# Decoder layer on one core: order of bank reads in the attention's reading cycles, and the last block's first steps placed inside the last attention cycles

## What is computed

```python
x = layernorm(x + attn(x))     # polynomial terms of a gate and a SwiGLU of width 1248
x = layernorm(x + xattn(x))    # 32 heads of width 128
x = layernorm(x + ffn(x))      # SwiGLU of width 1376

# xattn
h_q = rmsnorm(x) @ w_q.T; h_k = ctx @ w_k.T; h_v = ctx @ w_v.T
score = einsum('bqhd,bkhd->bhqk', h_q, h_k) + position_bias
score = softmax(where(mask, score, -inf))
out = x + einsum('bhqk,bkhd->bqhd', score, h_v) @ w_out.T

# ffn (the last block)
out = (silu(x @ Wg.T * ag) * (x @ Wu.T * au)) @ Wd.T * ad
```

## Time and profile before

| | |
|---|---|
| median of three runs | 755.46 us |
| the profiled execution's own time | 753.72 us |
| span of its profile (first to last instruction) | 751.9 us |
| TensorE busy | 716.2 us (95%), granted clock 0.992 on average |
| VectorE busy | 522.2 us (69%) |
| ScalarE busy | 408.6 us (54%) |
| GpSimd busy | 94.8 us (13%) |
| attention, from about | 206 to 612 us |
| last block, from | 613.1 us |

### The profile page before, as it was taken

How to read it: one execution, slowest core, us unless ns; L and a number is a source line. 1 busy time by engine, 2 the same in 40 slices (tenths; PEclk the granted TensorE clock), 3 DMA queues, 4 the chain that set the end, 5 groups by cost and what they waited for, 6 DMA issues and landing times.

```text
span 751.9 us, 12237 instructions
## 1 busy us (share of the span) xinstructions
PE 716.2 (95%) x4082; PEld 555.7 (74%) x4082; DVE 522.2 (69%) x848; ACT 408.6 (54%) x747; POOL 94.8 (13%) x88
## 2 busy tenths in 40 slices
PE   8999999999999999999999999999999779998993
PEld 6788888888878878776667787877656257886882
DVE  6555687588664875686876678667897828669565
ACT  6333323432355676776776666666676644454552
POOL 2000000074003600000000000000050004105403
PEclk9999999999999999999999999999999999999997
DMA  8455532545556765677997776668785513442631
GB/s 307 152 206 206 179 119 70 163 168 187 183 208 199 251 195 181 216 258 233 306 316 236 240 238 190 192 215 267 263 297 180 169 44 117 135 151 98 204 122 56
DMA packets 70681, 145.10 MB, mean 193 GB/s; under 512 B 7920, under 2 KB 8192, under 8 KB 69984
## 3 DMA queue, kind: packets, MB, share of 16 engines
q1 hardware_dynamic: 69200, 137.26, 55.7%
q0 software_dynamic: 1200, 6.70, 2.3%
q10 hardware_dynamic: 224, 0.39, 0.2%
HBM read 142.23 MB, written 2.10 MB: 192 GB/s over the span
## 4 chain that ended last, share of the span: by engine, by line
PE 86%; DVE 5%; issue 3%; DMA 2%; ACT 2%; POOL 1%; SPq 0%; ACTq 0%; DVEq 0%; POOLq 0%
PE bank L543 38%; PE acc L543 16%; PE acc L846 8%; PE bank L751 7%; PE bank L824 7%; PE bank L716 7%; PE bank L778 1%; PE bank L729 1%; DMA b_raw<-b 1%; DMA a_raw<-a 1%; PE bank L575 1%; DVE tile_lo L1288 1%; ACT v_sb L1186 1%; DVE a_lo L1288 1%; DMA wq<-wqn 1%
## 5 line engine op out<-in xcount | busy, mean ns | idle before, releaser
L543 PE MATMUL bank<-feat_hi,a_hi 128*128 128x512 f32 x348 | 137.7, 396 | 2.2 <-ACT u_sb L1193 0.8
L543 PE MATMUL bank<-feat_lo,a_hi 128*128 128x512 f32 x348 | 136.5, 392 | 2.1 <-issue 2.1
L1288 DVE TENSOR_TENSOR a_lo<-a_raw,a_hi 128x1024 fp32r<-128x1024 f32 (+3 forms) x47 | 56.8, 1208 | 94.5 <-ACT a_hi L1000 86.9
L543 PE MATMUL acc<-b_hi,tile_hi 128*128 128x512 f32 x224 | 87.8, 392 | 4.9 <-DVE tile_lo L1288 3.0
L543 PE MATMUL acc<-b_hi,tile_lo 128*128 128x512 f32 x224 | 87.3, 390 | 0.0
L543 PEld LDWEIGHTS bank<-feat_hi,a_hi 128*128 128x128 f32 x348 | 65.9, 189 | 22.6 <-issue 4.0
L543 PEld LDWEIGHTS bank<-feat_lo,a_hi 128*128 128x128 f32 x348 | 65.9, 189 | 13.5
L846 PE MATMUL acc<-u_sb,prob_t 32*128 32x512 f32 x512 | 73.0, 640 | 0.0
L543 PE MATMUL bank<-feat_hi,a_lo 128*128 128x512 f32 x180 | 70.1, 389 | 0.0
L1017 ACT ACTIVATE tile_hi<-pair 128x512 fp32r<-128x512 f32 x54 | 33.9, 628 | 66.3 <-DVE pair L1350 37.4
L751 PEld LDWEIGHTS bank<-t_ring,xn 128*128 128x128 f32 x512 | 62.1, 192 | 8.5 <-issue 7.2
(11 more groups left out here) (152 smaller groups left out, 1555.8 us busy)
## 6 DMA issues: line engine op xcount, KB each, us to landing
wqi<-ax SPq DMA_DIRECT2D x64, 256.0 KB, 3.3
wq<-wqn SPq DMA_DIRECT2D x64, 256.0 KB, 3.7
wv<-wvh SPq DMA_DIRECT2D x64, 256.0 KB, 4.0
wo<-bx SPq DMA_DIRECT2D x64, 256.0 KB, 4.0
a_raw<-w SPq DMA_DIRECT2D x22, 512.0 KB, 4.1
wk<-ax SPq DMA_DIRECT2D x43, 256.0 KB, 3.8
a_raw<-a SPq DMA_DIRECT2D x21, 512.0 KB, 5.4
b_raw<-b SPq DMA_DIRECT2D x34, 256.0 KB, 2.7
```

The costliest lines, as they stand in the source:

```text
L543: mm = pe.matmul(out_ap, w, x, start=start and k == 0, stop=stop and k == len(products) - 1, skip_group_check=True)
L1288: return dve.tensor_tensor(out_ap, whole, high, ALU.subtract)
```

## The change

Four things are done.
- In reading cycles TensorE's `values(n)` stands right behind `turn(n-1)` and no longer waits for `turned_ok`; ScalarE copies v_sb ahead of u_sb.
- `FEATURES_2` is HN - 6 = 58: the features' chunks 0, 1 and 2 stand in cycle 58, chunk 3 at the head of cycle 59, with their parts on ScalarE and VectorE. Since k_ring may still be in use, they are written to new tiles `last_hi`, `last_lo`, which share the addresses of ctx_raw1 and xn1 for half 0 and are feat_hi[1], feat_lo[1] for half 1.
- `gate(A30)` stands at the end of cycle 61 and `up(A30)` at the end of cycle 62, into bank 2 instead of bank 1. Silu follows in ScalarE's cycle 62, its split of weight tile A30 + 1 in cycle 61.
- SyncE loads A30 + 1 and T30 in cycle 58.

```diff
-FEATURES_1, FEATURES_2 = BLOCK - LEAD_T - 2, HN - 2
+FEATURES_1, FEATURES_2 = BLOCK - LEAD_T - 2, HN - LEAD_T
+GATE_30, UP_30 = HN - 3, HN - 2
...
# SyncE, at the end of a cycle
+                if n == FEATURES_2:
+                    sp.wait_ge(t_mm, HN)
+                    load_a(A30 + 1, (A30 + 1) % 2, w3[1][:, 0:2 * D])
+                    load_b(T30, T30 % 2, w3[0][:, 2 * D:])
-            sp.wait_ge(t_mm, HN)
...
# TensorE
-            def up(par, half, done, low=True):
+            def up(par, half, done, low=True, last=False, into=bank[1]):
                 pe.wait_ge(hidden_ok, done)
-                project(bank[1], par, 1, half, low=low).then_inc(a_used, 1)
+                project(into, par, 1, half, low=low, last=last).then_inc(a_used, 1)
...
# TensorE, values(n)
-                    else:
+                    elif shared(n) or not few:
                         pe.wait_ge(turned_ok, n)
...
# TensorE, a cycle
                     if n == HN:
                         weigh(n - 2)
-                        pe.wait_ge(feat_lo_ok, C)
-                        gate(A30, A30 % 2, 0, HALVES * F1)
+                    if n == FEATURES_2 + 1:
+                        features(2, 3, resid[:, TT:2 * TT, :], HN)
                     if n >= 1:
                         turn(n - 1)
+                    if few and late:
+                        values(n)
                     if 2 <= n < HN:
                         weigh(n - 2)
...
-                    if n >= FEATURES_2 and n < HN:
-                        features(2, 2 * (n - FEATURES_2), resid[:, TT:2 * TT, :], HN)
+                    if n == FEATURES_2:
+                        features(2, 0, resid[:, TT:2 * TT, :], HN)
...
                     if late:
                         outer(n - 1)
-                    if 0 <= n < HN:
+                    if 0 <= n < HN and not late:
                         values(n)
...
+                    if n == FEATURES_2:
+                        features(2, 1, resid[:, TT:2 * TT, :], HN)
...
+                    if n == GATE_30:
+                        pe.wait_ge(feat_lo_ok, C)
+                        gate(A30, A30 % 2, 0, HALVES * F1, last=True)
+                    if few and n == UP_30:
+                        pe.wait_ge(added_ok, HN)
+                        up(A30 % 2, 0, HALVES * F1, last=True, into=bank[2])
                     if few and 1 <= j <= 2 and 0 <= g and g + 1 < HALVES * GROUPS:
                         group_scores(g + 1, j - 1)
+                    if n == FEATURES_2:
+                        features(2, 2, resid[:, TT:2 * TT, :], HN)
...
                 pe.wait_ge(u_ok, HN)
-                up(A30 % 2, 0, HALVES * F1)
                 weigh(HN - 1)
...
# ScalarE, a cycle
+                if n == FEATURES_2 + 1:
+                    chunk(2, 3, bank[0])
                 if n >= 1:
                     copy_turned(n - 1)
...
-                if n >= FEATURES_2:
-                    chunk(2, 2 * (n - FEATURES_2), bank[0])
+                if n == FEATURES_2:
+                    chunk(2, 0, bank[0])
...
+                if n >= 0:
+                    copy_values(n)
                 if late:
                     copy_outer(n - 1)
-                if n >= 0:
-                    copy_values(n)
...
+                if n == FEATURES_2:
+                    chunk(2, 1, bank[0])
                 if 0 <= n + 1 < HN:
                     exponentials(n + 1)
+                if n == FEATURES_2:
+                    chunk(2, 2, bank[0])
...
+                if n == GATE_30:
+                    act.wait_ge(score_mm, HN)
+                    split_a(A30 + 1, (A30 + 1) % 2)
+                if n == UP_30:
+                    silu(A30, HALVES * F1, True, 0)
...
-            silu(A30, s0, True, 0)
+            split_b(T30, T30 % 2)
             copy_turned(HN - 1)
             copy_outer(HN - 1)
-            split_a(A30 + 1, (A30 + 1) % 2)
-            split_b(T30, T30 % 2)
...
# VectorE, a cycle
                 if 0 <= m < HN and m % GH > 0:
                     find_max(m)
+                if n == FEATURES_2:
+                    chunk(2, 0, bank[0])
+                if n == FEATURES_2 + 1:
+                    chunk(2, 3, bank[0])
                 if n >= 0:
                     divide(n)
...
-                if n >= FEATURES_2:
-                    chunk(2, 2 * (n - FEATURES_2), bank[0])
-                    chunk(2, 2 * (n - FEATURES_2) + 1, bank[0])
+                if n == FEATURES_2:
+                    chunk(2, 1, bank[0])
+                    chunk(2, 2, bank[0])
...
-            product(A30, s0, T30, T30 % 2, True, 0)
+            product(A30, s0, T30, T30 % 2, True, 0, second=bank[2])
```

More of the change, by code:

```diff
@@ L545, in passes, with project @@
                 return mm
-            def project(bank_, par, which, half, x_hi=feat_hi, x_lo=feat_lo, low=True):
+            def project(bank_, par, which, half, low=True, last=False):
+                x_hi, x_lo = (last_hi, last_lo) if last else (feat_hi, feat_lo)
                 for c in range(C):
@@ L576, in transposes, with gate @@
                 mm.then_inc(feat_mm, 1)
-            def gate(a, par, half, done, low=True):
+            def gate(a, par, half, done, low=True, last=False):
                 pe.wait_ge(a_lo_ok, a + 2)
                 pe.wait_ge(silu_ok, done)
-                project(bank[0], par, 0, half, low=low).then_inc(first_mm, 1)
-            def up(par, half, done, low=True):
+                project(bank[0], par, 0, half, low=low, last=last).then_inc(first_mm, 1)
+            def up(par, half, done, low=True, last=False, into=bank[1]):
                 pe.wait_ge(hidden_ok, done)
-                project(bank[1], par, 1, half, low=low).then_inc(a_used, 1)
+                project(into, par, 1, half, low=low, last=last).then_inc(a_used, 1)
             for h in range(HALVES):
@@ L899, in attention @@
                         down(T30 - 1, (T30 - 1) % 2, 1, last=True)
+                    if not few and late:
+                        values(n)
                     if late:
                         outer(n - 1)
-                    if 0 <= n < HN:
+                    if 0 <= n < HN and not late:
                         values(n)
@@ L954, in last_block @@
                 transposes(3, 1, bank[3], x1)
-                gate(a, a % 2, 0, s0 + f, low=low)
+                gate(a, a % 2, 0, s0 + f, low=low, last=True)
                 pe.wait_ge(feat_lo_ok, C + 1)
@@ L959, in last_block @@
                 transposes(3, 3, bank[3], x1)
-                up(a % 2, 0, s0 + f, low=low)
+                up(a % 2, 0, s0 + f, low=low, last=True)
                 down(T30 + f - 1, (T30 + f - 1) % 2, 5, low=low)
@@ L965, in last_block @@
                 a, t = A30 + F3, T30 + F3
-                gate(a, a % 2, 1, s0 + F3, low=low)
-                up(a % 2, 1, s0 + F3, low=low)
+                gate(a, a % 2, 1, s0 + F3, low=low, last=True)
+                up(a % 2, 1, s0 + F3, low=low, last=True)
                 down(t - 1, (t - 1) % 2, 5, last=True, low=low)
@@ L1341, in few_bias_rests, with product @@
                         few_bias_hi[:, part * GH:(part + 1) * GH, :].bitcast(F32)).then_inc(few_bias_ok, 1)
-            def product(a, done, m, mpar, last_block, f):
+            def product(a, done, m, mpar, last_block, f, second=bank[1]):
                 dve.wait_ge(silu_ok, done + 1)
```

39 lines of the change are left out of this document (22 added, 17 removed).

## The result

The changed kernel took 756.38 us (median of 20 runs, 754.73 to 757.92), the kernel before 755.32 (20 runs): ratio 1.0019, 95% interval 1.001 to 1.0028. The forecast was 753.4, at most 755.2. The profiled execution of after took 757.53 us (span 755.7), 1.2 over its median; that of before was 1.6 under its own. So the two traces lie 3.8 us apart, the medians 1.1. The granted clock of the changed kernel's 20 runs is 0.983 to 0.989 on average, and the profiled one stands at 0.983: it is one of those with the most time at half clock. I follow the traces and judge by the medians.

What follows compares the result with a forecast made beforehand. TensorE was taken as the bound (86% of the chain), VectorE full in cycles 48 to 52. Gains of 2.5 + 1.7, less 0.7 in the tail and 1.5 for the clock, gave 2.0 us: 753.4, range 751.6 to 755.2.

Steps and rivals of the forecast that it cites:

- the last block starting differently from before: Entry to the last block: a sign that would prove the prediction wrong; no change was forecast there.
- Term of 2.5 us for cycles 17 to 32: Cycles 17, 20, 21, 24 and 32: the early copy removes turn's wait for v_ok, five times 0.5 us.
- what is late next?: Reading cycles without the stall: TensorE's own work takes 3.1 us, and ScalarE's copies at 2.9 us just keep up.
- the `sem_inc` that the prediction named as free: Between queries and turn: the added sem_inc costs nothing, as others already stand there without a bubble.
- The second rival: Reading cycles: another wait, exponential chain or weight loads, replaces v_ok; gain about 0.2 to 0.7 us, time 755.0, chance 0.17.
- Term of 1.7 for cycles 53 to 57: Entering cycle 58: 0.7 us from the earlier exponential and k_ring copy, 1.0 from the stalls of cycles 56 and 57.
- Tail: Cycles 58 to 63, features, gate and up moved: loses 0.7 us, with a 3.2 us gap ahead of turn(60).
- the clock's 1.5: Cycle 61, behind the 3.2 us gap: 3.4 us at half clock cost between 0 and 1.7 us, taken as 1.5.
- The sentence on the clock: Cycles' idle gap: low clock is the default, activity lifts it; gain 2.0 us by this rule, 3.5 without.
- The rival "slower": From 593 on the clock stays down; if until weigh(63), it costs 7.5 us and gives 759.5, chance 0.06.

Runs made afterwards that it cites:

- experiments 6 and 8: 6: early copy without keys' idle wait, branch ahead of turn(63), on the kernel before, 748.08 us; 8: changed kernel, branch behind up in cycle 62, 749.63 us.
- Experiment 1: The changed kernel with the wait for u_ok in keys skipped where keys does nothing: 757.64 us, ratio 1.0028.
- experiments 7 and 9: 7: changed kernel, VectorE's feature chunks behind the divisions, 752.51 us, single run; 9: that plus keys' idle wait skipped and branch behind up, 746.19 us.
- experiment 4: The kernel before with the early copy of v_sb and without the u_ok wait where keys does nothing: 751.52 us, ratio 0.9961.
- filler kernel: The changed kernel with twelve matmuls that nobody reads added behind weigh(63): 753.17 us, ratio 0.9981.

## Why the prediction was wrong

- **The step that failed** is the one that had no term: "the last block starting differently from before" stands in the list of what would prove it wrong, and the sum took it at nothing. The text counted up's 2.95 us as work that fills idle time inside the cycles and never asked what those 2.95 us had covered where they stood. They had covered the flag's load and the branch. The timeline held the answer in its next line: the 0.67 us marked "issue" ahead of the gate was the visible end of a stretch of 4.76, from up's first matmul at 608.38 to the gate at 613.14. What the runs showed in its place is a stretch of 4.2 to 5.0 us that only queued matmuls hide; with the branch moved forward (experiments 6 and 8) the idle piece is gone and the time falls by 3.4 and about 7 us. How the stretch divides between the load of the flag, the branch and the fetch of code stays open. Price: 2.7 us by the first idle piece (4.49 against 1.81 from weigh(63) to the gate), and 1.2 between the gate and the mark (14.99 against 13.76), where the clock was low for 10 us instead of 3.4. Both are read from the two profiled executions, which lie further apart than the medians.
- **Term of 2.5 us for cycles 17 to 32**: mis-sized. From the turn of cycle 16 to that of cycle 32 the traces show 79.93 and 78.49 us, 1.44. The question "what is late next?" was answered by TensorE's own work; it was the wait in `keys`, right ahead of the `sem_inc` that the prediction named as free. Experiment 1 shows that. The second rival had said that another wait takes the place of `v_ok`; it was half right, with another wait than the ones it named. The weight loads that it named came next, once that wait was gone.
- **Term of 1.7 for cycles 53 to 57**: mis-sized too, 1.05. From turn(52) to turn(57) it is 23.05 and 22.00 us. (That VectorE ran without a gap from 533.97 on is right but for one piece of 0.16 us at 548.09.)
- **Tail**: right. +2.0 for +0.7 and the clock's 1.5; the idle piece 3.12 for 3.2, the wait at weigh(62) 0.78 for 0.9, one fall of the clock in cycle 61. The table load lay beside up and cost nothing.
- **The sentence on the clock**: the rule of the Trainium skill ("TensorE: Matmul & The Clock Gate", Part 1), that the low clock is the default and activity lifts it, was weighed at the cycles alone. The traces agree with it there, and at the entry too, where the same kind of piece (3.34 us) came with some 10 us at half clock, from 614 to 624. The rival "slower" had the clock as its mechanism, but at the wrong place, and it was not what began it.
- **The size at the end**: by the ratio the loss is 0.8 to 2.1 us, by the profiled executions 3.8. The difference of 2.7 is that of the two executions against their medians (1.60 and 1.15). Against the 751.7 us that the prediction gave for the profiled execution, the 757.53 are 5.8 too much: 3.9 at the entry, 1.6 in the cycles, 0.4 ahead of them, 0.1 behind the mark, less 0.2 in the tail.

## What to carry to other kernels

Before work is moved away from the end of a stage, look at what stands behind it on the same engine that shows no busy time: a flag's load, a branch, code that has to be fetched. A run-time branch on the critical engine goes where several microseconds of its work are already queued, at the price of having that work's code in both branches. And a removed wait is worth only what the next wait in program order lets through: read the code between the removed wait and the instruction, also where that code "does nothing".

## What the runs showed of the hardware

- TensorE's program runs ahead of its matmuls, by some 3 to 4 us at least (the matmuls of up and weigh, or of weigh and the filler): with twelve matmuls more between the last wait and the branch, the first matmul behind it came 4.77 us after that wait, not 3 us later.
- The clock's fall doesn't follow from the length of one idle piece. Pieces of 2.63 us and more ahead of turn(60) came with it in each of seven kernels. The same piece of 1.88 us was followed by 1.00 in the kernels of experiments 7 and 9 and by 0.50 in that with the keys' wait kept, and at the entry a piece of 2.38 us was followed by 1.00 in the kernel of experiment 4, one of 2.13 us by 0.50 in the kernel before. Slices of the kernel with the keys' wait kept:

```profile
591.00:592.00 1.00, 0.34 (x5) 1.00 0.57 217
592.00:593.00 1.00, 1.00 (x9) 0.54 0.03 8
593.00:594.00 1.00, 1.00 (x9) 0.50 0.00 0
```

- At half clock the matmuls of the last block's gate start 0.43 us apart, at full clock 0.23 (changed kernel, 619.44 to 623.71 and 624.76 to 626.14).
- The second idle piece at the entry (2.13 us before, 1.61 after, 2.59 with the early copy alone) is missing in the filler kernel and in those with the early branch. That it is the second transfer of code fits its place in the kernel before, but in the filler kernel two transfers lie between 612 and 616 as well and no such piece follows; why was not tried.
